# Attention stages with projections ahead of the second score passes, value products in halves, and norms a half stage earlier

## What is computed

```python
x = x + L0_attn(_layernorm(x), ...)              # gated recurrence, no attention
x = x + L0_xattn(_layernorm(x), ctx, ctx, ...)   # "cross": 16 heads of 8, rotated q and k
x = x + L0_ffn(_layernorm(x), ...)               # 16 routed experts and 2 shared
x = x + L1_attn(_layernorm(x), ...)              # "long" (plain) and "segment" (masked by segment), fused
x = x + L1_xattn(_layernorm(x), ctx, ctx, mask)  # "given": no projections, a mask that is given
x = x + L1_ffn(_layernorm(x), ...)               # 8 experts
# every attention:
scores = q @ k.T / sqrt(8); attn = softmax(scores); out = attn @ v
```

## Time and profile before

| | us |
|---|---|
| median of 3 runs | 522.71 (522.21 to 523.77) |
| the profiled execution, its own time | 521.07 |
| its span, first to last instruction | 519.3 |
| mean granted TensorE clock | 0.905 |
| busy: TensorE, VectorE, ScalarE, GpSimd | 424.1, 381.1, 264.1, 135.9 |
| cross attention | about 44 to 126 |
| long, segment and given attention | about 217 to 419 |

### The profile page before, as it was taken

The page is one execution under the profiler, slowest core; times in us unless marked ns, Lnnn a source line. Parts: engine busy times, 40 slices in busy tenths (PEclk is TensorE's granted clock), DMA queues, the critical chain, the costliest instruction groups (busy, mean ns, idle before and its releaser), DMA issues. The chain is left out here.

```text
span 519.3 us, 13895 instructions
## 1 busy us (share of the span) xinstructions
PE 424.1 (82%) x5548; PEld 281.2 (54%) x5548; DVE 381.1 (73%) x969; ACT 264.1 (51%) x393; POOL 135.9 (26%) x216
## 2 busy tenths in 40 slices
PE   1775888877768999778888888779979769999996
PEld 1343556654435666445566665544535436767675
DVE  5774568764498888837887979587666547999995
ACT  1151445532535776426655666343434537687772
POOL 4213112110245887512121211212021300131110
PEclk9988579977698999956989999789999989999999
DMA  7000010000001114000000000000000001112101
GB/s 256 0 1 9 2 57 3 4 3 0 1 18 36 54 45 152 1 1 3 1 3 4 3 3 3 2 1 23 21 3 2 3 0 42 43 42 55 68 1 42
DMA packets 9065, 13.08 MB, mean 25 GB/s; under 512 B 1450, under 2 KB 7474, under 8 KB 9010
## 3 DMA queue, kind: packets, MB, share of 16 engines
q1 hardware_dynamic: 9012, 12.32, 7.7%
HBM read 11.79 MB, written 0.52 MB: 24 GB/s over the span
## 5 line engine op out<-in xcount | busy, mean ns | idle before, releaser
L1282 DVE TENSOR_REDUCE smax<-sc 128x8 f32<-128x1024 f32 x64 | 77.9, 1219 | 34.6 <-PE sc L811 34.5
L581 ACT ACTIVATE probs<-sc 128x1024 f32<-128x1024 f32 x64 | 65.3, 1024 | 67.4 <-PE sc L811 67.4
L1549 DVE SCALAR_TENSOR_TENSOR x_all<-bk,comb,x_all 128x128 f32<-128x128 f32 x208 | 58.1, 342 | 1.5 <-PE bk L1133 1.3
L500 POOL TENSOR_TENSOR gated_lo<-gated,gated_hi 128x512 f16<-128x512 f32 x36 | 41.7, 1158 | 33.6 <-ACT gated_hi L655 33.6
L686 ACT ACTIVATE probs<-sc,w 128x512 f32<-128x512 f32 x64 | 40.6, 686 | 14.1 <-PE sc L1110 14.0
L860 PE MATMUL bk<-probs,v_pad 128*32 128x128 f32 x1024 | 40.7, 305 | 8.5 <-ACT probs L581 4.6
L1655 DVE TENSOR_TENSOR p_lo<-probs,p_hi 128x1024 f16<-128x1024 f32 x32 | 38.3, 1223 | 3.1 <-ACT p_hi L693 2.6
L1297 DVE RECIPROCAL inv_sum<-bk 128x128 f32<-128x128 f32 x32 | 30.3, 948 | 13.5 <-PE bk L867 13.5
L867 PE MATMUL bk<-probs,ones_pad 128*32 128x128 f32 x1024 | 40.0, 305 | 0.0
L811 PE MATMUL sc<-qmT,qkT 32*128 32x128 f16 x512 | 26.0, 223 | 16.8 <-DVE smax L1282 16.5
L860 PEld LDWEIGHTS bk<-probs,v_pad 128*32 128x32 f32 x1024 | 30.1, 121 | 15.3 <-issue 12.9
(11 more groups left out here) (247 smaller groups left out, 1041.3 us busy)
## 6 DMA issues: line engine op xcount, KB each, us to landing
w<-in_w SPq DMA_DIRECT2D x8, 514.0 KB, 4.0
w<-in_w SPq DMA_DIRECT2D x18, 192.0 KB, 2.4
wd<-in_wd SPq DMA_DIRECT2D x1, 644.0 KB
x_all<-in_x SPq DMA_DIRECT2D x1, 512.0 KB, 4.1
ctxT<-in_ctx_t SPq DMA_DIRECT2D x4, 128.0 KB, 3.1
ctx_tok<-in_ctx SPq DMA_DIRECT2D x4, 128.0 KB, 2.2
mask_in<-in_mask SPq DMA_DIRECT2D x4, 128.0 KB, 2.6
out<-x_all SPq DMA_DIRECT2D x1, 512.0 KB, 3.2
```

Source lines behind the costliest of these rows:

```text
L500: pool.tensor_tensor(gated_lo[:, k % DEPTH, :], gated[:, k % DEPTH, :], gated_hi[:, k % DEPTH, :], ALU.subtract).then_inc(c_glo, 1)
L581: act.activation(probs[:, n % 2, half, :], sc[half][:, :], ACT.Exp, scale=HD ** -0.5).then_inc(u_exp, 1)
L1282: dve.tensor_reduce(smax[:, s, 8 * half:8 * half + 8], sc[half][:, :].rearrange("p (h k) -> p h k", k=S), X, ALU.max).then_inc(u_max, 1)
L1549: op = dve.scalar_tensor_tensor(x_all[:, bb, :], (bk4, bk5)[k % 2][:, b * 128:(b + 1) * 128], w, x_all[:, bb, :], ALU.mult, ALU.add)
```

## The change

On TensorE, `normed` moves ahead of the first `scores_T` of a stage. The projections (`inputs`) of long and segment pairs move ahead of `scores_T(q, 1, 0)` in the first half and of `scores_T(p, 0, 0)` in the second, which are the passes that wait for the first maxima of the half. `numerators` and `sums` become `values(n, s, half, r)`: for one half of the heads the value products and then the sums, then the same for the other half, and `stack_maxima` comes after all of them. In the second half of a stage `outputs` or `late_projections` stand between the two halves of the value products. On ScalarE the copy of `xnT` goes ahead of the first `exp`. On VectorE and GpSimd `norm_stats` with what belongs to it (`start_norm`, `finish_norm`) moves to the first half of the stage, except where `late` is set, and `norm_apply` moves to right behind the maxima of the second half; `inputs_given` moves to the first half too. `xn` gets more slots (`slot_of`), and the DMA of a mask no longer waits for the values of an earlier pair.

```diff
...
 def slot_of(p):
-    return 2 if p.kind == "given" and p.i % 2 == 0 else 0
+    return (4 if p.kind == "given" else 0) + 2 * (p.i % 2)
 def place(n):
...
     def load_pair(i):
+        if i >= 2:
+            sp.wait_ge(e_any, 3 * (i - 2) + 1)
+        sp.dma_start(mask_in[:, i % 2, :, :], A["mask"][i]).then_inc(ld_mask[i % 2], 16)
+        if i >= 2:
+            sp.wait_ge(u_vpad, given(i - 2).n + 2)
         sp.dma_start(ctx_tok[:, i % 2, :, :], A["ctx"][i]).then_inc(ld_ctx[i % 2], 16)
-        sp.dma_start(mask_in[:, i % 2, :, :], A["mask"][i]).then_inc(ld_mask[i % 2], 16)
     load_pair(0)
     load_pair(1)
     for e in range(2):
         sp.dma_start(w1[:, e, :], A["w1"][e]).then_inc(ld_w1[e], 16)
     for i in range(2, B // 2):
-        sp.wait_ge(u_vpad, given(i - 2).n + 2)
-        sp.wait_ge(e_any, 3 * (i - 2) + 1)
         load_pair(i)
...
+    def finish_norm(nxt):
+        at = slot_of(nxt)
+        rsqrt((LN_B if nxt.kind == "cross" else LN_D) + nxt.norm, 2, at=at)
+        if nxt.kind == "given":
+            pool.wait_ge(e_any, 3 * nxt.i + 3)
+            pool.tensor_tensor(rstd_any[:, at:at + 2], rstd[:, at:at + 2], mask_any[:, :, 1], ALU.mult)\
+                .then_inc(e_q, 1)
     def stage(r, p, q, nxt=None, late=None, ahead=None, last=None):
         if p:
             copy_values(p, 0)
         if r:
             split_low(r, 0)
+        if nxt and not late:
+            finish_norm(nxt)
         if p:
             copy_values(p, 1)
         if ahead:
...
         if ahead == LN_F:
             weights1_low(0, 0)
             weights1_low(1, 1)
-        if nxt:
-            at = slot_of(nxt)
-            rsqrt((LN_B if nxt.kind == "cross" else LN_D) + nxt.norm, 2, at=at)
-            if nxt.kind == "given":
-                pool.wait_ge(e_any, 3 * nxt.i + 3)
-                pool.tensor_tensor(rstd_any[:, at:at + 2], rstd[:, at:at + 2], mask_any[:, :, 1], ALU.mult)\
-                    .then_inc(e_q, 1)
+        if nxt and late:
+            finish_norm(nxt)
         if r:
             split_low(r, 1)
...
     def stage(r, p, q, nxt=None, late=None, ahead=None, last=None):
-        if q:
-            exp(q.n + 1, 1)
         if r and r.kind in ("cross", "long"):
             evac_xT(xnT[:, :], bk5[:, 0:256], (XT_B if r.kind == "cross" else XT_D) + r.i + 1)
         if q:
+            exp(q.n + 1, 1)
             exp(q.n + 1, 0)
         if r and r.kind == "cross":
             values_in(r, 0)
...
                               ident_h[:, :])
         mm.then_inc(u_qm_ps, 1)
-    FROM_LAST = tuple(reversed(range(J)))
-    def numerators(n, s, r):
-        pe.wait_ge(u_vpad, n + 1)
-        if n >= 1:
-            pe.wait_ge(u_norm, n)
-        if r and r.kind == "cross":
-            pe.wait_ge(v_sb, r.n + 2 - s)
-        for i in FROM_LAST:
-            if i % 2 == 1:
-                pe.wait_ge(u_exp, 2 * n + 2 - i // 2)
+    def products(s, half, dst, table):
+        for i in (2 * half + 1, 2 * half):
             for g in range(G):
                 c = slice((i % 2 * G + g) * 128, (i % 2 * G + g + 1) * 128)
-                pe.matmul(AV[32 * g:32 * g + 32, :], v_pad[:, s, g, 32 * i:32 * i + 32],
-                          probs[:, s, i // 2, c], start=i == J - 1, stop=i == 0)
-    def sums(n, s):
-        for i in FROM_LAST:
-            for g in range(G):
-                c = slice((i % 2 * G + g) * 128, (i % 2 * G + g + 1) * 128)
-                mm = pe.matmul(SUMS[32 * g:32 * g + 32, :], ones_pad[:, 32 * i:32 * i + 32],
-                               probs[:, s, i // 2, c], start=i == J - 1, stop=i == 0)
-        mm.then_inc(u_av, 1)
+                mm = pe.matmul(dst[32 * g:32 * g + 32, :], table(g, 32 * i), probs[:, s, half, c],
+                               start=dst is AV and i == J - 1, stop=i == 0, skip_group_check=True)
+        return mm
+    def values(n, s, half, r):
+        own_v = lambda g, at: v_pad[:, s, g, at:at + 32]
+        own_one = lambda g, at: ones_pad[:, at:at + 32]
+        if half == 1:
+            pe.wait_ge(u_vpad, n + 1)
+            if n >= 1:
+                pe.wait_ge(u_norm, n)
+            if r and r.kind == "cross":
+                pe.wait_ge(v_sb, r.n + 2 - s)
+        pe.wait_ge(u_exp, 2 * n + 2 - half)
+        products(s, half, AV, own_v)
+        mm = products(s, half, SUMS, own_one)
+        if half == 0:
+            mm.then_inc(u_av, 1)
     def normed(r):
         if r.kind == "cross":
             if r.i:
                 pe.wait_ge(rope_rd, r.n)
-            transposes(bk5[:, 0:256], XN_B + r.n, 2)
+            transposes(bk5[:, 0:256], XN_B + r.n, 2, at=slot_of(r))
         else:
             if r.i:
                 pe.wait_ge(qkv_sb, 4 * r.i)
-            transposes(bk5[:, 0:256], XN_D + 2 * r.norm, 2)
+            transposes(bk5[:, 0:256], XN_D + 2 * r.norm, 2, at=slot_of(r))
     def inputs(r, s, q):
...
     def stage(r, p, q, nxt=None, late=None, ahead=None, last=None):
         if p:
             scores(p, 0, 0)
+        if r and r.kind in ("cross", "long"):
+            normed(r)
         if q:
             scores_T(q, 1, 1, p)
         if p:
             stack_T(p, 1)
-        if r and r.kind in ("cross", "long"):
-            normed(r)
         if late:
             late_transposes(late)
+        if r and r.kind != "cross":
+            inputs(r, 0, q)
         if q:
             scores_T(q, 1, 0, p)
         if p:
             scores(p, 0, 1)
-        if r:
+        if r and r.kind == "cross":
             inputs(r, 0, q)
-            if r.kind == "segment":
-                segments(r)
+        if r and r.kind == "segment":
+            segments(r)
         if q:
-            numerators(q.n + 1, 1, r)
+            values(q.n + 1, 1, 1, r)
+            values(q.n + 1, 1, 0, r)
         if p:
             stack_maxima(p, 0, True)
-        if q:
-            sums(q.n + 1, 1)
         if late:
             late_fusion(late)
...
             scores_T(p, 0, 1, True)
         if r:
             stack_T(r, 0)
+            if r.kind != "cross":
+                inputs(r, 1, q)
         if p:
             scores_T(p, 0, 0, True)
             scores(p, 1, 1)
-        if r:
+        if r and r.kind == "cross":
             inputs(r, 1, q)
+        if p:
+            values(p.n, 0, 1, r)
         if q and q.kind == "segment":
             late_projections(q, r)
         elif q and q.kind != "long":
             outputs(q)
         if p:
-            numerators(p.n, 0, r)
+            values(p.n, 0, 0, r)
             stack_maxima(p, 1, r)
-            sums(p.n, 0)
         if ahead:
             transposes(bk5[:, :], XN_OF[ahead], 4, at=4)
     pe.wait_ge(ready, 4)
...
             dve.wait_ge(u_qm_ps, n - back + 1)
         split_high(r, s)
+    def start_norm(nxt):
+        if nxt.kind == "given":
+            masks_given(nxt)
+            dve.wait_ge(x_done, OUT_D + nxt.i + 1)
+        norm_stats(2 * nxt.i, 2, (LN_B if nxt.kind == "cross" else LN_D) + nxt.norm, at=slot_of(nxt))
     def stage(r, p, q, nxt=None, late=None, ahead=None, last=None):
         if p:
             maxima(p, 0, 0)
...
         if r and r.kind == "segment":
             segment_rows(r)
             counts(r)
+        if r and r.kind == "given":
+            inputs_given(r)
+        if nxt and not late:
+            start_norm(nxt)
         if ahead:
             if ahead == LN_C:
                 dve.wait_ge(x_done, 4)
...
             maxima(p, 1, 1)
         if ahead:
             norm_apply(0, 4, ahead, at=4)
+        if nxt and late:
+            start_norm(nxt)
         if nxt:
+            at, scale = slot_of(nxt), rstd
             if nxt.kind == "given":
-                masks_after = r if r and r.kind == "given" else None
-                if masks_after:
-                    inputs_given(masks_after)
-                masks_given(nxt)
-                dve.wait_ge(x_done, OUT_D + nxt.i + 1)
-            norm_stats(2 * nxt.i, 2, (LN_B if nxt.kind == "cross" else LN_D) + nxt.norm, at=slot_of(nxt))
-        elif r and r.kind == "given":
-            inputs_given(r)
+                dve.wait_ge(e_q, nxt.i + 1)
+                scale = rstd_any
+            norm_apply(2 * nxt.i, 2, (LN_B if nxt.kind == "cross" else LN_D) + nxt.norm, at=at, scale=scale)
         if r:
             inputs_high(r, 1)
         if r and r.kind == "long":
...
             if q:
                 dve.wait_ge(d_short, q.i + 1)
             alone(r)
-        if nxt:
-            at, scale = slot_of(nxt), rstd
-            if nxt.kind == "given":
-                dve.wait_ge(e_q, nxt.i + 1)
-                scale = rstd_any
-            if r and r.kind == "segment":
-                dve.wait_ge(d_lx, 9 * r.i + 9)
-            norm_apply(2 * nxt.i, 2, (LN_B if nxt.kind == "cross" else LN_D) + nxt.norm, at=at, scale=scale)
         if q and q.kind in ("cross", "given"):
             outputs(q)
         if last:
```

4 lines of the change are left out of this document (2 added, 2 removed).

## The result

The changed kernel took 528.4 us in the middle of four runs (526.57 to 538.96), the kernel before, on the same chip in the same minutes, 522.46 (518.49 to 523.77). The ratio is 1.0127, its 95% interval [1.0067, 1.0188]: slower by some 6.6 us, and outside the range of 518.5 to 526.5. One thing must be known to read the numbers: executions of one and the same kernel here differ by which stretches run at half clock, so that a kernel's runs spread over 3 to 20 us, and ratios are taken without the most disturbed ones.

A forecast was written before the change was run, and what follows sets the result against it. No engine binds everywhere: a loop bounds cross and given halves, VectorE segment stages. Cross +3.3, long -1.6, segment +1.4, stage 1 +0.7, given -3.45, emptying -1.1 sum to -0.75: profiled 520.3, median 522.0 us, range 518.5 to 526.5.

The forecast's parts named there:

- Long stages: Stages 2, 4, 6: sums fill the transposes' wait in first halves, second halves stay; -0.6, -0.6 and -0.4, sum -1.6 us.
- Cross stages: Later transposes and casts, a wait for the copy of v, later first-half casts; +3.3 us over stages 1 to 4.
- the third term: Cross stage 3, first half: casts end later than the next maximum stood, +0.25 us.
- the other two: Cross stage 3, second half: late transposes with casts behind them, +0.6; value products waiting for ScalarE's copy of v, +0.63.
- Segment stages: Stages 3, 5, 7: VectorE work moves into gapless first halves, late projections delay `short_rows`; -0.5, +0.9, +1.0, sum +1.4 us.
- Stage 1: Filling the second loop, where the projection now precedes a score pass nobody holds up: +0.7 us.
- Given stages: Stages 8 to 12, no projection: the transposes' wait shrinks, against casts behind late transposes; sum -3.45 us.
- Emptying: Last value products wait for the first `exp`; half the sums run while the second is computed: -0.55 twice, -1.1 us.
- The first: Rival: faster, a half-clock spell near 326 to 332 us goes; 520.3, or 519.5 with a second; chance 0.22.
- the third: Rival: slower, the cast's wait also holds the stacks' transposes, 0.5 for each of 6 halves, 525 us; chance 0.07.
- the second: Rival: slower, new gaps in cross 2, stages 8 to 9, 10 to 11 bring 1.7 us spells; 525.4; chance 0.28.
- The rule weighed: TensorE drains at tiling-mode changes, one or two more per stage: up to 2 us higher, 524; not adopted, chance 0.05.

The follow-up runs named there:

- the products: kernel before with only the value products by halves, transposes of the maxima behind all, outputs or late projections between: 528.87 us, ratio 1.0066.
- the norms alone: kernel before with only the norms' part (norm_stats in the first half, norm_apply behind the second half's maxima): 527.76 us, ratio 1.0136.
- the projections' part: kernel before with only the projections of long and segment pairs and the norm's transposes moved earlier: 529.56 us, ratio 1.0155.

## Why the prediction was wrong, point by point

**Long stages, the term that failed: -1.6 predicted, +2.45 measured, 4 of the 6.4 us between forecast and result.** Two sentences of it were wrong. "so the projection gains only 0.1 there", in the first half: it loses 1.23 in stage 4 when alone and 0.50 with the products by halves, since the score pass behind it, ScalarE's `exp`, its copy of the stacks and so the transposes all come later. The value products did start where the sum had them (2.63 behind M, for 2.57); the transposes, for which the sum had no wait, start 0.48 too late, and that is what the half missed (-0.11, for -0.6). I followed TensorE's own next wait (for the quotient) and not the engine whose input was delayed. "The second half of a long stage is VectorE's own and stays": VectorE had no gap there, and the copy of qkv came just in time; 0.85 later it held the casts up. These halves, booked at nothing, lost 3.0 of the 4.05: 0.76 in stages 4 and 6, and 1.48 in stage 2, where VectorE did have a gap, at its second maxima. The product part of the term, -0.6, came out when the products stood alone (-0.61).

**Cross stages: right in mechanism and in the sum, less so in the terms.** +3.3 predicted, +3.0 at full clock. The waits for the late transposes and for the copy of v are both found by the runs. But in stage 3 the third term, +0.25 in the first half, was 0.02, and the second half lost 1.55 for the 1.23 of the other two; that the stage came to +1.56 for +1.5 is luck in part. The 0.8 in stage 2's first half shows only when all parts are together (8.13, against 7.29 with the products and 7.08 with the norms alone); how much of it is the norm's and how much that of the earlier `normed` (7.75 at 0.96 with the projections' part) no run separates.

**Segment stages: right in mechanism, too small.** First half of 5 as forecast (+0.73, for 0.8), `short_rows` as forecast. In stage 3 I booked -0.5 for a half that was at 0.77 of the clock; at full clock the first half costs 0.78. In stage 7 the masks and the norm cost 1.57 of the 1.7 in the first half; what the second half gives back is not seen, since it ran at 0.80 of the clock (8.72, for 8.12 at full clock). Stage 1, booked at +0.7, lost 1.11 in the profile.

**Given stages: -3.45 predicted, -4.4 at full clock (without stage 12's second half), -1.5 in the profile.** Stages 10 to 12 gained 0.2 to 0.5 more each than forecast, and stage 8 1.0 more. In stage 9 the first half costs 1.88, not 1.1; that the casts ahead of the masks are themselves late is my explanation and not tested. The second half returns 1.17. Stages 8, 9 and 11 in the profile show -3.18, +3.29 and +0.99; the difference from the full-clock column is clock. Emptying, and stage 12's second half: everything behind stage 12's first half was 0.8 shorter in the profile, for 1.0 forecast.

**The rivals.** The first came true in part (stage 8's first half 6.83 at full clock instead of 9.55 at 0.64, but 3.4 of the 6.8 us at half clock moved into the half before), the third in small (0.22 by the late transposes of the stacks, for 0.5), and the second came true at the places it named: cross stage 2, stages 8 to 9 and 10 to 11. Its price was wrong: 1.7 a spell, where cross stage 2 lost 4.2 (12.83 against 8.68) and stage 11 2.3 (8.82 against 6.51). The first of these spells lasted 10.2 us, and the price was that of one half's products and sums. Together the first two rivals cancel in the sum over the program (47.8 against 49.5 us of clock). The full-clock column (cross +2.98, long +2.45, segment +3.06, given -4.38) with stage 1's 1.11 as profiled and the 0.8 by which everything behind stage 12's first half was shorter makes +4.4 of order for the +6.6 measured; the rest I can't assign between segment 7's second half, spells and the runs' own spread.

**The rule weighed.** The rows chosen against it had no idle time, but they did hold the cost: start to start, each change between split and unsplit matmuls takes some 0.1 us, before and after, which agrees with the drain that the Trainium skill names (TensorEngine Tiling, Key Properties); that it is the drain and nothing else at these seams no run separates. And the prediction counted wrong: the new order has 40 such changes fewer, not one or two more in a stage, so the rule pointed to a gain, by an estimate from these numbers of up to 4 us of TensorE's time, of which only what is on the path counts.
